# A fused graph-convolution and expert-routing kernel: the prefix sums earlier in the turn, the router's last part woven with a root, and roots of 11 links

## The reference, cut to what matters

```
x = x + graph_conv(_gn(x))     # layer 0
x = x + experts(_gn(x))        # layer 1
```

## Time and profile before

| | |
|---|---|
| time, median of 3 runs | 679.85 us (679.73 to 680.88) |
| the profiled execution's own time | 677.07 us |
| its span, first to last instruction | 675.2 us |
| outside the span | 1.9 us |
| PE, DVE, ACT, POOL busy | 79%, 59%, 35%, 32% of the span |
| PE's mean granted clock | 0.903 of full speed |
| chain that ended last | PE 49%, DVE 32%, DMA 8%, issue 7% |

### The profile page before, as it was taken

The page is one execution under the profiler, slowest core; times in us unless marked ns, Lnnn a source line. Parts: engine busy times, 40 slices in busy tenths (PEclk is TensorE's granted clock), DMA queues, the critical chain, the costliest instruction groups (busy, mean ns, idle before and its releaser), DMA issues.

```text
span 675.2 us, 11949 instructions
## 1 busy us (share of the span) xinstructions
PE 533.8 (79%) x2664; PEld 358.1 (53%) x2665; DVE 399.5 (59%) x1697; ACT 239.0 (35%) x603; POOL 216.7 (32%) x283
## 2 busy tenths in 40 slices
PE   0468489999999989989883319999999999998233
PEld 0233257776666666666662205666666665665122
DVE  4654326798898888888889753333333333332265
ACT  0343044444444444444331202333333333333232
POOL 5000000324444444444445521434334343344000
PEclk9988689999999999999986559999999999999555
DMA  9900000000000000000000142222222222220696
GB/s 293 428 23 1 0 1 1 1 0 33 33 33 33 31 33 33 32 32 33 32 32 33 55 128 63 86 79 90 82 88 81 86 89 83 91 85 28 205 312 229
DMA packets 36259, 52.85 MB, mean 78 GB/s; under 512 B 4605, under 2 KB 31360, under 8 KB 35968
## 3 DMA queue, kind: packets, MB, share of 16 engines
q1 hardware_dynamic: 24816, 30.86, 14.6%
q0 software_dynamic: 6480, 16.85, 6.7%
q10 hardware_dynamic: 4928, 4.72, 2.1%
HBM read 30.19 MB, written 23.14 MB: 79 GB/s over the span
## 4 chain that ended last, share of the span: by engine, by line
PE 49%; DVE 32%; DMA 8%; issue 7%; ACT 2%; POOL 1%; SPq 1%; DVEq 0%; ACTq 0%; POOLq 0%
PE bank L615 18%; PE bank L630 9%; DVE vq L1000 4%; PE bank L492 4%; DMA out<-xT 4%; PE bank L377 3%; PE bank L602 2%; PE bank L623 2%; DVE work L1177 2%; DVE work L1161 2%; PE bank L459 2%; DVE vq L999 2%; DMA xs<-x_in 2%; PE bank L367 2%; DVE work L1212 1%
## 5 line engine op out<-in xcount | busy, mean ns | idle before, releaser
L615 PE MATMUL bank<-w,xT 128*128 x284 | 135.5, 600 | 2.1 <-DVE xT L1405 2.1
L1405 DVE COPY xT<-bank 128x256 f32<-128x256 f32 x71 | 30.2, 425 | 143.6 <-PE bank L602 143.6
L966 POOL DMA_INDIRECT yrows<-xT,dest x71 | 69.5, 980 | 138.7 <-ACT xT L822 132.5
L492 PE MATMUL bank<-work 128*128 128x256 f32 x384 | 97.7, 396 | 0.0
L935 POOL DMA_INDIRECT xrows<-xtok,slot x64 | 67.2, 1050 | 78.9 <-DVEq L1298 61.7
L492 PEld LDWEIGHTS bank<-work 128*128 128x128 f32 x384 | 70.3, 195 | 9.4 <-issue 1.0
L923 POOL TENSOR_TENSOR yg<-work,sml 128x512 f32<-128x512 f32 x16 | 18.0, 1123 | 177.7 <-DVE work L1212 177.7
L630 PE MATMUL bank<-w,xT 128*128 x284 | 73.3, 380 | 1.6 <-ACT xT L827 1.6
L615 PEld LDWEIGHTS bank<-w,xT 128*128 128x128 f32 x284 | 48.9, 192 | 37.5 <-issue 37.5
L816 ACT ACTIVATE xT<-bank 128x256 f32<-128x256 f32 x71 | 27.3, 384 | 95.5 <-PE bank L615 95.5
L630 PEld LDWEIGHTS bank<-w,xT 128*128 128x128 f32 x284 | 48.5, 190 | 6.2 <-issue 2.5
(11 more groups left out here) (200 smaller groups left out, 977.8 us busy)
## 6 DMA issues: line engine op xcount, KB each, us to landing
xT<-xrows SPq DMA_DIRECT2D x71, 129.0 KB
xT<-yrows SPq DMA_DIRECT2D x32, 256.0 KB, 4.0
xs<-x_in SPq DMA_DIRECT2D x4, 1024.0 KB, 11.3
w<-w13t_in SPq DMA_DIRECT2D x1, 4096.0 KB, 18.0
out<-xT ACTq DMA_DIRECT2D x16, 256.0 KB, 3.9
w<-w2t_in SPq DMA_DIRECT2D x1, 2048.0 KB, 22.3
yrows<-xT,dest POOLq DMA_INDIRECT x71, 2.4
xrows<-xtok,slot POOLq DMA_INDIRECT x64
```

The costliest lines, as they stand in the source:

```text
L492: last = mm(bank[6][:, h * N:(h + 1) * N], z[:, p, c, k, h], A[:, p, c, k], start=(c == 0 and k == 0), stop=(c == C - 1 and k == K - 1))
L615: last = mm(bank[2 + q][:, :], xc[:, q, c], w13[:, e, c].rearrange("p w n -> p (w n)"), start=(c == 0), stop=(c == C - 1))
L966: pool.indirect_dma_start(yrows, bass.IndirectOffsetOnAxis(ap=dest[:, q], axis=0), yo[:, q], None, bounds_check=2 * TOKENS - 1, oob_is_err ...
L1405: V.tensor_copy(xc[:, q].rearrange("p c k -> p (c k)"), bank[q][:, 0:C * P]).then_inc(c_xc, 1)
```

## The change

1. PE: `prefix` moves from the end of the turn to a place ahead of `product`. It no longer waits for `b_nb`, but for `v_gq` at a value that the first link of the group norm's root (L1206, which takes the variance out of the PSUM bank) reaches.
2. `reciprocal_root` loses two links: instead of three Newton steps there is one step of third order (4 links) and one Newton step (4 links), so that a root has 11 links with its first. All three kinds of root use it.
3. DVE: the last weave is split in another way. `layer_norm`, `choose` and `weigh` are woven with `group_norm` only along; what is left of `group_norm` is woven with `route_c` and with `add_bs`, which comes after a pause of three rounds.

```diff
@@ prefix
-                pe.wait_ge(s["b_nb"], done(min(b + 1, B - 1) if isinstance(b, int) else b + 1))
+                pe.wait_ge(v_gq, ROOT * min(b + 1, B - 1) + 1)
                 pe.wait_ge(s["b_M"], done(b))
@@ PE's turn
                 if ahead1:
                     features(i + 1, 1 - q, 0)
+                if back3:
+                    prefix(i - 3, 1 - q)
                 if ahead2:
                     product(i + 2, q)
                 if now:
                     conv(i, q)
                 if ahead1:
                     features(i + 1, 1 - q, 1)
-                if back3:
-                    prefix(i - 3, 1 - q)
@@ reciprocal_root, with THIRD = 0.375 ** 0.5
-                for last in (False, False, True):
...
+                yield from step.then(V.scalar_tensor_tensor(out=v[:, 2], in0=guess, scalar=THIRD, in1=v[:, 0], op0=ALU.mult,
+                                                            op1=ALU.mult))
+                yield from step.then(V.tensor_tensor(v[:, 3], v[:, 2], guess, ALU.mult))
+                yield from step.then(V.scalar_tensor_tensor(out=v[:, 2], in0=v[:, 3], scalar=-1.25 / THIRD, in1=v[:, 3],
+                                                            op0=ALU.add, op1=ALU.mult))
+                yield from step.then(V.scalar_tensor_tensor(out=guess, in0=v[:, 2], scalar=1.875, in1=guess, op0=ALU.add,
+                                                            op1=ALU.mult))
+                yield from step.then(V.tensor_tensor(v[:, 2], v[:, 0], guess, ALU.mult))
+                yield from step.then(V.scalar_tensor_tensor(out=v[:, 3], in0=v[:, 2], scalar=-0.5, in1=guess, op0=ALU.mult,
+                                                            op1=ALU.mult))
+                yield from step.then(V.scalar_tensor_tensor(out=v[:, 2], in0=v[:, 3], scalar=0.5, in1=guess, op0=ALU.add,
+                                                            op1=ALU.mult))
+                yield from step.then(V.tensor_tensor(guess, guess, v[:, 2], ALU.add))
@@ norm, ln_roots, gn_roots (ROOT = 11)
-                step = Steps(dve, a_hv, g, 16)
+                step = Steps(dve, a_hv, g, ROOT + 3)
-                step = Steps(dve, v_lq, b, 13)
+                step = Steps(dve, v_lq, b, ROOT)
-                step = Steps(dve, v_gq, b, 13)
+                step = Steps(dve, v_gq, b, ROOT)
@@ DVE's turn
-                def matrices():
+                def weighing():
                     if ahead1:
                         yield from pause(10)
                         yield from weigh(i + 1, 1 - q)
+
+                def adding():
                     if ahead2:
+                        yield from pause(3)
                         yield from add_bs(i + 2, q)
...
-                weave(variance, group_norm(), matrices(), choice)
-                weave(router(route_c))
+                group = group_norm()
+                weave(variance, choice, weighing(), along=(group,))
+                weave(group, router(route_c), adding())
```

More of the change, by code:

```diff
@@ L68 @@
 MAGIC = 1597463007.0
+ROOT = 11
+THIRD = 0.375 ** 0.5
 def done(b):
```

## The result

| | before | after |
|---|---|---|
| median of 11 runs | 679.73 us (677.25 to 681.83) | 684.13 us (680.30 to 688.41) |
| profiled execution, its span | 677.07, 675.2 us | 682.0, 680.2 us |
| PE, DVE busy | 79%, 59% | 78%, 58% |
| a full turn, most of them | 17.15 us | 17.48 us |
| eleven full turns | 189.92 us | 195.93 us |

The ratio is 1.0069, 95% interval 1.0046 to 1.0092: slower by 4.4 us, where I had forecast 12.65. The direction is the one forecast and the time lies in the range, near its lower end; the rise forecast was almost three times the measured one.

What follows compares the result with a forecast made beforehand. It took the image stage's chain, mostly through DVE, as the bound, and after the change a loop through all engines. Terms 7.4 + 0.5 + 8.0 - 1.75 - 1.5 = +12.65 took 679.85 to 692.5 us, range 682 to 699.

Steps and rivals of the forecast that it cites:

- PE's clock: Pauses of 2.23 us ahead of `logits` would drop PE to half clock in five of eleven full turns: +8.0 us.
- The price of a fall: Half clock on PE for some 3 us behind `logits` would lengthen that turn by 1.6 us.
- The loop: Chain `ln_c`, `add_bs`, `logits`, `turn_softmax` and back: 17.83 against 17.15 us per turn, +7.4 us over eleven full turns.
- add: Distance on DVE from the start of `ln_c` to `add_bs` in a full turn: 7.09 us instead of 4.41.
- Turn 2: Turn of the image stage with the same new DVE order but without a router: +0.5 us.
- Opening: First two roots, now with fewer links, while PE waits for both: gains of 1.33 and 0.42 us, together -1.75 us.
- Last turns: Turns 16 to 18: the router's last part runs inside the root instead of behind it, -1.5 us.
- The clock stays: Rival: PE's granted clock does not fall in the pauses of the full turns; 684.5 us, chance 0.25.
- Faster, since a held link slips through: Rival: L1002 on DVE is not held by POOL, `add_bs` starts at 6.21 us, turn 0.2 shorter; 674.3 us, chance 0.12.

Runs made afterwards that it cites:

- filled_mid: Changed kernel plus three calls of useless matmuls in PE's pause ahead of `logits`, only in turns 3 to 13: 678.82 us, 1.0022 to before.
- after_again: The changed kernel timed and profiled once more, nothing altered: 683.33 us, 1.0090 to before.
- opening_root: Kernel before with the new root of 11 links in the opening (`norm`) alone: 677.35 us, 0.9992 to before.
- gate: Changed kernel with POOL's `ln_out` also waiting for the third link of the group norm's root (L1000): 670.29 us, 0.9893 to before.
- prefix_late: Changed kernel with `prefix` back at the end of PE's turn, its wait on the root's first link kept: 693.94 us, 1.0249 to before.

## Why the prediction missed its size

- **PE's clock, +8.0: the step that failed.** The price of a fall was right (1.6 forecast, 1.57 measured), and so was the mechanism. The number of falls was a guess between none and eleven. Five were taken; two profiles show two each, and filled_mid prices them at 3.2 to 4.6 us by the ratios. The pause was 1.94 us and not 2.23. The term was too large by 3.4 to 4.8 us in the median, 4.9 in the profiled execution.
- **The loop, +7.4: the other step that failed, mis-sized by as much.** Path and waits came as forecast: L548 (now L550) without a wait, L461 behind the tanh, DVE waiting at L1210, L999 and L1002 held for 0.99 and 0.97, L1003 held to the end of POOL's third. The terms were each a little long: add 6.88 and not 7.09, 8.38 and not 8.46, 0.83 and not 0.89; together 0.35 per turn. Since the term is a difference of two near numbers (17.83 less 17.15), 2% too much in the loop doubled it: 0.33 per turn was left of 0.67. Over the eleven turns filled_mid, which has the loop without falls, is 2.85 us above before, not 7.4: too large by some 4.5. (Eleven times 0.33 would be 3.6; the kernel before has irregular turns too, of 17.71, 17.45 and 17.52.) The prediction counted the held links of the new order without those of the old: before, L1000 is held for 1.12 and again for 0.57 us in each full turn, so that of the three held links now (0.99, 0.97, 0.56) only L1002's 0.97 is new. It did not need them for the sum, which goes by the distances.
- **Turn 2, +0.5:** turns 1 and 2 together took 29.23 instead of 28.83, +0.4.
- **Opening, -1.75:** the first image was normalised at 24.01 instead of 26.16, but 0.8 of that is an earlier arrival of data: the first statistic stands at 9.21 instead of 10.01. From it to the first normalised image it is 14.80 us instead of 16.15, also in after_again and opening_root (14.79): 1.35 less, the 1.33 forecast. How much of it reaches the end can't be told; the time of opening_root differs from before by -0.5 us (-2.2 to +1.2).
- **Last turns, -1.5: wrong in sign.** From turn 16's first `centre` (360.42 before, 363.54 after) to the router's last instruction (L1295 at 389.24, L1299 at 392.92) it took 29.38 instead of 28.82 us, and 29.40 and 29.51 in after_again and filled_mid: +0.6. Turn 16 is 1.3 us shorter, but turns 17 and 18 are 1.9 us longer. The term looked at the router's last part only. In turn 17 of before the group norm's scale is finished ahead of that part (L1239 at 380.84, L1285 at 381.39), in the changed kernel near its end (L1243 at 384.53, L1289 at 383.59), so that ACT's output for the next `tokens` comes later, and with it the next choice. PE and DVE in turn 18, before and after:

```profile
382.18 1.03 PE L529 MATMUL bank<-xn,sml 128*8 128x128 f32 x8 [0.83 <-ACT xn L772]
384.41 0.21 DVE L1250 COPY xtok<-tok 128x2 f32<-128x2 f32 x1 [1.59 <-PE bank L541]
```

```profile
385.86 1.03 PE L531 MATMUL bank<-xn,sml 128*8 128x128 f32 x8 [2.58 <-ACT xn L774]
388.09 0.17 DVE L1254 COPY xtok<-tok 128x2 f32<-128x2 f32 x1 [3.05 <-PE bank L543]
```

  Turns 14 and 15, which lie ahead of these, took 32.78 us before with two falls of the clock, and 32.68, 31.39 and 29.74 in the changed kernel, filled_mid and after_again with two, one and none: there the clock makes the difference.
- **The rivals.** "The clock stays" gave 684.5, which is the measured median to 0.4 us, but for the wrong reason: the clock did fall, and the loop cost less. "Faster, since a held link slips through" gave 674.3; in the changed kernel L999 and L1002 were held in every full turn of both profiles, so it did not occur there, and in gate, where later POOL lets links through, 670.3 was measured. That add came at 6.19 there, with 6.21 forecast, is partly luck: the rival let L1002 through between two POOL instructions with L999 held, and the first `weigh` at 2.34 us; in gate both pass ahead of POOL's first instruction, `weigh` starts at 1.40, and a later link (L1010) is held instead.

Taken together: filled_mid, the change without falls in full turns, is 1.5 us above before. By the traces the loop and turn 2 make 3.3 of that and the last turns 0.6, which leaves -2.4 for the opening, where I had -1.75. That figure is a remainder, unsure by as much, and was not measured by itself. So the forecast was too high by two terms of some 4 us each, the number of falls and the loop, and a gain of 1.5 that did not come made up for a part of that.

## What to carry to other kernels

Before weaving two chains to hide one, ask what stands behind them: an instruction whose result another engine needs for the next turn (`add_bs` here) belongs ahead of the weave, and one move of it was worth 20 us beside the 4.4 at stake, with 3 of the 20 from PE's clock. The same holds for the result that was finished late by the new weave (the group norm's scale in turns 17 and 18). Where a loop runs through several engines, its length is a sum of distances read from the trace; five kernels followed it to 0.02 us, as long as that loop was the slowest. A predicted difference of two such sums should carry the error of both, and a mechanism that falls in some turns and not in others should be given as a range and tested by taking it away, not by counting once. One profile is one run: stages that nobody changed differed by up to 4 us between profiles here, as much as the whole effect.

## What was not expected of the hardware

After the same pause PE's clock falls in some turns and not in others: of the ten `logits` between 153 and 314 us in the first profile, all behind pauses of 1.93 to 2.09 us, two ran at half clock, in the second profile two other ones. The Trainium skill ("TensorE: Matmul & The Clock Gate", "Why this matters for your kernels") asks to avoid idle gaps on PE that are longer than any pause in the full turns here. The traces show falls behind 1.94 us and, in turn 15 of the kernel before, behind 1.71, so the page's bound does not keep this kernel at full clock. No full turn of gate fell behind 1.27 us, six of eleven in prefix_late behind 2.60, and filling 1.56 us of the changed kernel's pause, so that 0.44 was left, removed the falls in the full turns.

A few hundredths of a microsecond in the start of a POOL instruction decide whether a DVE instruction of 0.17 us takes 1.12: POOL at 0.77 and L999 at 0.80 us after `ln_c` hold it, POOL at 1.03 does not. The Trainium skill ("SBUF — State Buffer", "Who interferes with whom") says that the order of issue decides who blocks, which these rows bear out: a later start of POOL, 32% busy and 1% of the chain that ended last, bought 12 us, some 3 of them through the clock.
